# Layer 0's attention: four scores of a step one by one, maxima and products with v between them

## The reference

```python
qkv = x @ W_attn + b_attn                       # x is the layer-normed input
att = einsum('bhtd,bhsd->bhts', q, k) / sqrt(8) + alibi_causal_mask
att = softmax(att)
y = einsum('bhts,bhsd->bhtd', att, v)           # then y @ W_proj + b_proj
```

## Time and profile before

| | |
|---|---|
| median of 3 runs | 549.77 us (549.62 to 553.83) |
| the profiled execution | 550.55 us, its span 548.8 us |
| PE busy | 453.5 us, 83% of the span |
| DVE busy | 359.2 us, 65% |
| ACT busy | 241.2 us, 44% |
| POOL busy | 181.3 us, 33% |

### The profile page before, as it was taken

How to read it: one execution, slowest core, us unless ns; L and a number is a source line. 1 busy time by engine, 2 the same in 40 slices (tenths; PEclk the granted TensorE clock), 3 DMA queues, 4 the chain that set the end, 5 groups by cost and what they waited for, 6 DMA issues and landing times.

```text
span 548.8 us, 8788 instructions
## 1 busy us (share of the span) xinstructions
PE 453.5 (83%) x3228; PEld 175.3 (32%) x3228; DVE 359.2 (65%) x598; ACT 241.2 (44%) x471; POOL 181.3 (33%) x285
## 2 busy tenths in 40 slices
PE   7796788888788787877796887888998999889786
PEld 3262122131222222222332532333433334234332
DVE  5778668777788787876254686684487367732550
ACT  2574477867776778777566012421011111111120
POOL 3032506170313222222101262685067206930400
PEclk9997789998999999999796898899999999979999
DMA  7622332314102020200000132120022013100000
GB/s 220 230 66 66 114 119 67 103 42 186 37 2 66 2 65 2 66 2 3 3 0 2 57 134 78 39 77 1 29 106 78 1 57 116 39 0 1 20 1 19
DMA packets 19086, 31.79 MB, mean 58 GB/s; under 512 B 2544, under 2 KB 7120, under 8 KB 18724
## 3 DMA queue, kind: packets, MB, share of 16 engines
q1 hardware_dynamic: 19044, 31.23, 17.6%
HBM read 13.20 MB, written 8.06 MB: 39 GB/s over the span
## 4 chain that ended last, share of the span: by engine, by line
PE 61%; DVE 10%; ACT 10%; DMA 6%; issue 6%; SPq 4%; POOL 1%; ACTq 0%; DVEq 0%; POOLq 0%
PE PS L670 9%; ACT prob L1396 7%; PE PS L828 7%; PE PS L652 6%; PE PS L785 6%; PE PS L872 5%; PE PS L811 5%; DMA k_op<-k_scr 4%; DVE pmax L1081 4%; SPq L472 3%; PE PS L844 3%; PE PS L584 3%; PE PS L858 3%; PE PS L588 2%; DVE sm L1239 1%
## 5 line engine op out<-in xcount | busy, mean ns | idle before, releaser
L1081 DVE TENSOR_REDUCE pmax<-PS 128x8 f32<-128x1024 f32 x144 | 171.9, 1222 | 49.5 <-PE PS L584 33.4
L1396 ACT ACTIVATE prob<-PS 128x512 f32<-128x512 f32 (+1 forms) x320 | 159.9, 552 | 72.9 <-PE PS L652 70.0
L1541 POOL TENSOR_SCALAR_AFFINE_SELECT prob<-prob 128x512 f32<-128x512 f32 x64 | 40.0, 637 | 179.1 <-ACT prob L1396 179.1
L652 PE MATMUL PS<-q_op,k_op 55*128 55x512 bf16 (+3 forms) x384 | 61.7, 342 | 43.9 <-ACT prob L1396 41.1
L670 PE MATMUL PS<-prob,vaug 128*16 128x512 f32 (+3 forms) x768 | 83.8, 526 | 0.0
L1572 POOL TENSOR_TENSOR vdec<-vk,c_sb 128x256 f32<-128x256 f32 x56 | 33.0, 622 | 104.5 <-ACT vk L1420 104.4
L584 PE MATMUL PS<-k_op,q_op 52*128 52x128 bf16 (+3 forms) x576 | 58.6, 279 | 8.7 <-DVE pmax L1081 4.5
L1463 ACT COPY oT<-PS 128x512 f32<-128x512 f32 x32 | 17.5, 589 | 109.1 <-PE PS L844 93.8
L1239 DVE TENSOR_TENSOR sm<-PS,c_sb 128x512 f32<-128x512 f32 x64 | 41.2, 685 | 33.0 <-PE PS L811 32.4
L652 PEld LDWEIGHTS PS<-q_op,k_op 55*128 55x128 bf16 x384 | 18.4, 94 | 125.5 <-ACT prob L1396 109.3
L811 PE MATMUL PS<-qr,kr 64*128 64x512 f32 x128 | 36.3, 644 | 13.6 <-DVE sm L1239 10.4
(11 more groups left out here) (181 smaller groups left out, 493.4 us busy)
## 6 DMA issues: line engine op xcount, KB each, us to landing
turned<-by_sin SPq DMA_DIRECT2D x80, 128.0 KB, 2.0
k_op<-k_scr SPq DMA_DIRECT2D x14, 220.0 KB
q_op<-q_scr SPq DMA_DIRECT2D x14, 208.0 KB
c_sb<-const_dram SPq DMA_DIRECT2D x1, 2572.0 KB, 8.4
q_scr<-part_a SPq DMA_DIRECT2D x6, 256.0 KB, 3.4
k_scr<-part_a SPq DMA_DIRECT2D x6, 256.0 KB, 3.8
q_scr<-part_b SPq DMA_DIRECT2D x6, 256.0 KB, 3.4
k_scr<-part_b SPq DMA_DIRECT2D x6, 256.0 KB, 3.8
```

Source lines behind the costliest of these rows:

```text
L652: last = mm(PS[:, (GH * s + h) % ST_BANKS, at:at + nn], k_op[rows, slot, h // 2, P * j:P * j + P], q_op[rows, slot, h // 2, P * i0:P * i0 ...
L1081: vec.tensor_reduce(pmax[:, of_pair, at:at + step * (TPS - 1) + 1:step], both.rearrange("p a (b c) -> p a b c", c=P), AX.X, ALU.max).then_ ...
L1396: sca.activation(prob[:, s % P_SLOTS, h, 0:UNIT_W[u]], PS[:, k % ST_BANKS, 0:UNIT_W[u]], ACT.Exp).then_inc(s_exp, 1)
L1541: po.affine_select(out=blk, in_=blk, compare_op=ALU.is_ge, fill=0.0, base=0, pattern=[[0, GH], [1, P]], channel_multiplier=-1).then_inc(s_ ...
```

## The change

The loop of a step is written in another order. Before: scores of heads 0 and 1, first items, scores of heads 2 and 3, second items, then the whole product with v of the step before. Now: score 0, first items, score 1, first piece of the product, score 2, second items, score 3, second piece. The product is cut by columns: a unit with one key tile into two halves, a unit with two key tiles into its two tiles. The waits of the product (the exponentials and the diagonal of the step before, the copy of bank 7) stand at the first piece; its signal at the second. In an item the odd heads' matmul now comes before the even heads'.

```diff
--- before.py
+++ after.py
@@ -579,7 +579,7 @@
                     elif u == 0:
                         pe.wait_ge(s_op[slot], OP_EACH * (n // OP_SLOTS + (slot > 0)))
                     for t, (i, j, nb, at) in enumerate(ROUNDS[r]):
-                        for odd in range(2):
+                        for odd in (1, 0):
                             rows = rows_of(odd, MAX_K)
                             last = mm(PS[:, ring + odd, P * at:P * (at + nb)], q_op[rows, slot, pair, P * i:P * i + P],
                                       k_op[rows, slot, pair, P * j:P * (j + nb)], start=(t == 0), stop=(r not in DIAGONALS),
@@ -655,23 +655,27 @@
                             last.then_inc(s_st, 1)
                     at += nn
 
-            def pv(s):
+
+            def pv(s, piece):
                 n, u = divmod(s, NU)
                 b, g = GROUPS[n]
                 half, segs = UNITS[u]
-                pe.wait_ge(s_exp, GH * (s + 1))
-                pe.wait_ge(s_tri, TRI[s])
-                if u in (0, 3):
-                    pe.wait_ge(s_acc, 1 + 2 * n + (u == 3))
-                at = 0
-                for j, i0, nn in segs:
+                if piece == 0:
+                    pe.wait_ge(s_exp, GH * (s + 1))
+                    pe.wait_ge(s_tri, TRI[s])
+                    if u in (0, 3):
+                        pe.wait_ge(s_acc, 1 + 2 * n + (u == 3))
+                j, i0, nn = segs[0]
+                pieces = segs if len(segs) == 2 else [(j, i0, nn // 2), (j, i0 + nn // 2 // P, nn // 2)]
+                at = pieces[0][2] if piece else 0
+                for j, i0, nn in pieces[piece:piece + 1]:
                     c0 = P * i0 - SPAN * half
                     for h in range(GH):
                         last = mm(PS[STRIP * h:STRIP * h + VW, 7, c0:c0 + nn], vaug[:, TPB * b + j, g * GH + h, :],
-                                  prob[:, s % P_SLOTS, h, at:at + nn], start=(j == 0),
+                                  prob[:, s % P_SLOTS, h, at:at + nn], start=(j == 0 and piece == 0),
                                   stop=(u in (2, 9)), skip_group_check=True)
-                    at += nn
-                last.then_inc(s_pv, 1)
+                if piece:
+                    last.then_inc(s_pv, 1)
 
             def unit_b(k, part):
 
@@ -723,11 +727,13 @@
                 beside = items_of_step(s) if s < NSTEP else ()
                 for half in range(2):
                     if s < NSTEP:
-                        scores(s, range(GH // 2 * half, GH // 2 * (half + 1)))
+                        scores(s, [GH // 2 * half])
                     for k in (beside[:len(beside) // 2], beside[len(beside) // 2:])[half]:
                         item(k)
-                if s:
-                    pv(s - 1)
+                    if s < NSTEP:
+                        scores(s, [GH // 2 * half + 1])
+                    if s:
+                        pv(s - 1, half)
 
 
             pe.wait_ge(s_exp, GH * NSTEP)
```

## The result

The changed kernel takes 564.4 us, median of four runs (561.43, 563.98, 564.84, 566.2), against 550.4 before: ratio 1.0237, 95% interval 1.0174 to 1.0300. The other three executions took 2.6 to 4.8 us more, at a mean granted clock of 0.952 to 0.954 instead of 0.958; they have no trace. All ratios compare the fast executions of either kernel, the kernel before having been run again beside the experiments, so a ratio is not the quotient of the medians next to it (1.0237 here rests on four executions of the kernel before, of 549.6 to 553.8 us, where those beside the experiments went down to 541.6).

What follows compares the result with a forecast made beforehand. Layer 0's attention was taken as bound by a repeating chain: PE and ACT loops, then DMA waits. Six rounds at +1.54 (+9.2) and the last group (+1.2) gave 561.0 profiled, 560 us predicted, range 549 to 569.

Steps and rivals of the forecast that it cites:

- Stretch P: From k_op's landing to the first mrow DMA (units 9, 0, 1): 7.45 us instead of 6.75, +0.70 per round.
- Stretch Q: From the first mrow DMA to unit 3's first score: engines end last at 5.17 us, DMA needs 4.43, +0.74.
- Stretch R: From unit 3's first score to the next mrow DMA: unit 4's gain used up by waiting for bank 7's copy, +0.1.
- Stretch T: From that mrow DMA to the next k_op landing, set by SP and DMA: stays at 9.86 us, 0.
- Six rounds: Group 0's unit 9 to group 6's unit 5: each group's round 1.54 us longer, six times, +9.2 us.
- First group: The attention's first group, set by DVE's maxima, two or three a half step: no change, 0.
- Last group: Last transposes now stand ahead of step 79's score 3, adding score, exponential and POOL: +1.2 us.
- The open cost: Lone scores beside item matmuls: taken as 0; upper bound 0.21 us per lone score, +6.5 us, 567 in all.
- The waits did not fall into slack: Rival: first piece's waits end before PE comes, Q stays DMA-set, only P's +0.70 remains: 554 us, 19%.
- the shorter loop: Rival: POOL and copy stay hidden, five 512-column steps of P and R run at 2.29 us: 537 us, 12%.
- The clock's fall: Rival: PE's waits up to 1.4 us in units 1, 2, 9 lower the clock: +6 to +9, 566 to 569 us, 10%.

Runs made afterwards that it cites:

- the version that the rest points to: Kernel before with odd matmul first, score pairs in the first three steps, then one by one, product uncut at the step's end: 544.4 us, ratio 0.9911.
- the run with pairs: Changed kernel with scores in pairs ahead of the items again, as before, the product still in two pieces: 547.1 us, ratio 0.9925 to the kernel before.
- the matmuls that serve nothing: Eight unused 512-column matmuls ahead of each k_op wait, added to the one-by-one, whole-product kernel: 549.1 us; with pairs in the first three steps too: 546.5 us.

## Why the prediction was right

**Forecast and sum.** Slower, 560 us, range 549 to 569: 564.4 lies inside, 4 us over. The sum was made for the profiled execution, 561.0, and that took 561.4. The rest of the distance is between executions, which I had not allowed for beyond 0.8 us: the profiled one was the fastest of four. That the sum meets the profiled execution within 0.5 us is in part luck, as the terms below show.

**Stretch P, +0.70:** 7.45 forecast, 7.45 measured. Score 1 behind the diagonal item, POOL before the first piece of unit 9, the diagonal item before score 3 of unit 0, each within 0.15 us of the working.

**Stretch Q, +0.74:** 5.17 forecast, 5.28 measured, set by the two POOL instructions as said; without them it is 4.44.

**Stretch R, +0.1:** measured -0.14, so mis-sized by 0.25. The product of unit 3 did wait for the copy of bank 7 (0.64 us), but the first pieces came earlier than I had them: unit 2's at 0.99 us for 1.13, unit 3's at 3.47 for 3.66, and unit 5's first score at 5.12 for 5.34.

**Stretch T, 0:** measured -0.3. PE's wait for k_op stayed at 0.77 us where I had 1.4. In the two chains SP's loads went out faster and landed later (one issue took 0.35 us for 1.51 before, and the landing 5.52 for 4.68), 0.3 us less in all. That is within T's spread.

**Six rounds, +9.2:** measured +7.7. **First group, 0:** measured +1.65; pairs put back there, in the version that the rest points to, give 1.6. **Last group, +1.2:** measured +2.0. The transposes in the last steps, which the term was made of, come to +0.7 there; units 1 to 6, which I put at nothing, lost 2.8; and unit 0 gained 1.3, where the clock of the kernel before was 0.58. From 260 to 304 us the granted clock was 1.00 here and 0.81 there, so at a like clock the last group would have lost more. Ahead of the last group stand -1.2 and in layer 1 +0.7 that no term had. Five errors of 0.7 to 1.65 us, of both signs, cancel in the sum; that is luck.

**The open cost, 0 to 6.5 us:** 0, as taken. But my reason, and the Trainium skill's rule as I read it ("TensorE: Matmul & The Clock Gate", Part 3), gave the order of the two matmuls the credit; turned round, it costs nothing: 563.9 us, where the upper bound with even heads first was 569 to 573. Score and item have two passes for each half of the array in either order, and that count is what the rows agree with. Whether weights are loaded under a running matmul of the same rows no run here shows by itself.

**What was wrong in the reasoning.** I listed the waits of the first piece and the scores behind items as two costs to be added, and expected to be rid of only 0.3 to 0.4 us by pairs. In P they are no sum: the wait for POOL costs 0.7 us where what it holds up includes a diagonal item and behind it the last score, and next to nothing (0.08) where the last score stands ahead of that item; the late score costs nothing (0.04) where no piece waits for the last exponential. In Q it is nearer to a sum: behind unit 1's two POOL instructions the pieces cost 0.6 us with pairs and 0.85 without. The working by times had all of this in it; it was the list of costs, and the run with pairs that I expected from it (559 to 563 us, measured 547.1), that had it wrong.

**Signs.** Line 1541, now 1547, has PE waiting for it, and unit 3's first score waits for no DMA, as said. A lone score and its item start together, as in the rows of unit 4's step (224.03). Landing to landing is 29.67 us for 30.1. Two signs failed: PE waits 0.77 us for k_op, not 1.4, and the steps of units 6 and 7 take 3.05 and 2.20 us, not 2.3 to 2.4. For those steps I had left out that unit 6 has a diagonal item in its first half, ahead of score 1.

**Rivals.** The waits did not fall into slack in Q, and the shorter loop did not decide: it is there in unit 7's step (2.20 us for 2.75), but that step lies in T. The clock's fall did not come at the new waits of 1.3 us in this kernel's profile (full clock from 82 to 304 us); it came in other kernels behind waits for k_op. Over all profiles here it fell behind 13 of the 24 waits for k_op of 1.23 to 2.50 us, and behind none of the 24 shorter ones. The Trainium skill's rule (same page, Part 1) that idle stretches lower the clock agrees with the rows at 0.57, and the matmuls that serve nothing kept the clock up; but waits of 1.86 and 2.15 us with the full clock behind them show that the wait alone does not decide, and what else does is open.

## What to carry to other kernels

When an instruction with a wait moves up an in-order queue, write down the loop that it closes: what it waits for, and everything behind it that produces that thing for the next round. A wait and a late producer may each be nearly free and cost together; test them apart before either is given up. Where a DMA sets a stretch, a faster stretch beside it only lengthens the wait, behind which the clock may fall. And before two totals are compared, look at the granted clock in the part that is the same in both: here layer 1, the same in two kernels, took 4.8 us more at 0.94 than at 0.97.

## What the runs showed of the hardware

- Which half of the array an item's first matmul uses makes no difference to two lone scores around it: 0.54 us to the next product in both orders.
- Products of 512 columns in one piece or in two pieces one behind the other give the same P, Q and R to 0.01 us; apart, a piece of 256 columns takes 0.56 us.
- The granted clock fell to 0.50 to 0.71 of full speed in the 4 us behind 13 of 24 waits of PE for k_op of 1.23 to 2.50 us, with P longer by 1.1 to 1.5 us, and by 2.1 and 2.4 us where it was at half for the whole 4 us. Eight matmuls in that wait kept it at full speed in all eight rounds that have it.
- Layer 1, with the same 1168 matmuls, took 250.0 us at a mean granted clock of 0.94 and 245.2 at 0.97, in two executions.
- POOL's instruction on a 128x512 block took 0.634 to 0.641 us, and PE's matmul behind it started 0.14 us after its end.
- One execution of the same kernel differs from another by more than I had thought: 541.6 to 556.0 us in 25 runs of the kernel before.
